# A fused transformer block: the mixing rounds issue in another order, and each chunk's rows are scattered a round later

## The chip, the cores and the metric

One core of one Trainium2 chip. The metric is the device time of one execution in microseconds (us). In the profile PE is TensorE (PEld its weight loads), DVE is VectorE, ACT is ScalarE, POOL is GpSimd and SP is SyncE.

## What is computed

The block has four layers, each with a residual and a layer norm before and after. The input is 32 sequences of 256 positions with 128 features. Cut to what matters:

```
x = x + ln(attention(ln(x)))            # 16 heads, causal, with a bonus per key
x = x + ln(wide(ln(x)))                 # 128 -> 512 gated, 512 -> 512 gelu, 512 -> 512 gelu, 512 -> 128
x = x + ln(recurrence(ln(x)))           # h = tanh(x_t Wi + bi + h Wh + bh) along axis 1
x = x + ln(experts(ln(x)))              # shared expert + one routed expert of 32

def wide(x):
    h = silu(x @ w1 * s1) * (x @ w2 * s2)
    h = gelu(h @ h1 * t1); h = gelu(h @ h2 * t2)
    return h @ w3 * s3

def experts(x):
    shared = silu(x @ sg) * (x @ su) @ sd
    logits = x @ gate_w
    owner, score = argmax(logits), sigmoid(max(logits))
    routed = swiglu of owner(x * score)
    return shared + routed
```

## The kernel before

The program has three stages: attention (to about 900 us in the trace), the mixing rounds (to about 1732 us), and the expert slots. The change touches only the second.

**Chunks and rounds.** The mixing stage (`mixing_experts`) works on 16 chunks of 512 rows (NC = 16, CHUNK = 512, four tiles of 128 rows, CT = 4). Every engine runs 21 rounds, k = 0 to 20 (`rounds`): eight written out, eight as a hardware loop of two, five written out. A round holds several chunks at once, each at another stage, and its arguments are their numbers: p = k is normed for the wide layer, a = k-1 goes through its first, gated layer, c = k-2 through its two 512 x 512 layers and the output, v = k-3 through the recurrence, h = k-4 through the norm behind the recurrence and the third residual sum, q = k-5 through the router, the shared expert and the placing of its rows. A letter is None where there is no such chunk. Rounds 5 to 15 hold all of them; round 16 has no p, round 17 no a, round 18 no c, round 19 no v, round 20 no h.

**Order of the work.** There is no scheduler. Each engine runs its own list in the order in which the code is written, and waits on semaphores. A wait holds up everything behind it on the same engine.

**PE in a round.** The four quarters of c's first 512 x 512 layer (`first_layer(0)` to `first_layer(3)`, L1228, L1230, L1237: 12 products of 128 x 512 each, the last four on the rounding remainder hT_low) are mixed with small things: the turning of xn4 (L1197, waits for ACT's copy of the state before it, hs), the router's logits (L1265), the shared expert's gate and up products in two halves (`shared(0)`, `shared(1)`, L1254), the turnings of xn2 and xn3 (L1197 too), the shared expert's down product (L1293), the recurrence's input product (L1300) and the counts for the placing (L1306 to L1311). `shared(1)` waits until DVE has emptied the two PSUM banks of `shared(0)`:

```
wait(pe, s["shid"], IC * q + m)
```

Behind that come, for each quarter m, a's first layer (L1322 to L1325) and c's second layer with 16 recurrence steps between the products (L1204), then the output (L1338) and the turning of the recurrence's state (L1350), which ends the round on PE.

**DVE in a round.** It starts with the norm of xn2 left from the end of the round before (L1519, chunk p), then for v: y (L1543), its statistics (L1510, L1514), its normed form (L1519, waits for POOL's brs_y), the second residual x (L1551) and its statistics. Then `shared(0)` (L1534, L1538: shid), xn2T_low (L1558), the norm of x (xn3, L1519), `shared(1)`, and the router's argmax (L1571 to L1582). The second half of the round holds the gated products (L1679, L1685), the gated rows, the norm of hs, the third sum (L1660), `place` (21 small instructions, L1616 to L1642), xn4, the statistics of x1c and the low parts (L1647).

**POOL in a round.** It makes one over the square root of the variance for each norm (`rstd`: L1144 scales, L1146 raises to -0.5), the rounding remainders of the gelu's output (`low_part`, L1139, four a round, for c's second layer) and, at the end, the scatter of q's rows to their places in DRAM (L1167: four indirect DMAs, one per tile). The scatter waits for the places, the gated rows and the shared expert's output of chunk q:

```
for k in range(CT):
    pool.indirect_dma_start(out=sorted_d[:, :], out_offset=bass.IndirectOffsetOnAxis(
        ap=pos_i[par][:, k:k + 1], axis=0), in_=row_buf[1 - par][:, k, :], in_offset=None)\
        .then_inc(s[f"placed{1 - par}"], 16)
```

`row_buf` has two buffers; DVE's third sum (L1660) writes the one that chunk h shares with chunk h-2, and waits until that chunk's rows are placed.

**ACT in a round.** Copies of the turned tiles out of PSUM (xn4T L1443, xn2T_high L1448, xn3T L1455, hs L1487), the gelu of each quarter (`middle`, L1423 and L1424), the tanh of the shared expert (L1430), the copy of its output (L1458) and of the router's top (L1463), and in the second half the tanh, gelu and recurrence steps (L1468, L1479, L1414). SP loads x1c and x1v and, in round 18, the experts' weights.

Of the kernel before, what the change touches and what calls it, by code (L numbers as in the profile page):

```python
# [906 lines left out]
def mixing_experts(nc, early, x1_d, mix, wgu, row_buf, sorted_d, gate_up, down, sh_gate_up, sh_down, out):  # L907
# [6 lines left out]
    with ExitStack() as ctx:  # L914
# [109 lines left out]
        def rounds(eng, step):  # L1024
            def row(k, par):
                return [v if not isinstance(v, int) or 0 <= v < NC else None for v in
                        (k, k - 1, k - 2, k - 3, k - 4, k - 5)] + [par]
# [44 lines left out]
        def _(sp):  # L1072
# [3 lines left out]
            def step(p, a, c, v, h, q, par):  # L1076
# [39 lines left out]
        def _(pool):  # L1116
# [31 lines left out]
            def step(p, a, c, v, h, q, par):  # L1148
# [5 lines left out]
                low_part(c, 1)  # L1154
                low_part(c, 2)
                low_part(c, 3)
# [5 lines left out]
                if q is not None:  # L1162
                    wait_apart(pool, s["pos"], q + 1, s["const"])
                    wait_apart(pool, s["rows"], q + 1, s["const"])
                    wait_apart(pool, s["sh_out"], q + 1, s["const"])
                    for k in range(CT):
                        pool.indirect_dma_start(out=sorted_d[:, :], out_offset=bass.IndirectOffsetOnAxis(  # L1167
                            ap=pos_i[par][:, k:k + 1], axis=0), in_=row_buf[1 - par][:, k, :], in_offset=None)\
                            .then_inc(s[f"placed{1 - par}"], 16)
# [24 lines left out]
        def _(pe):  # L1194
# [14 lines left out]
            def step(p, a, c, v, h, q, par):  # L1209
# [45 lines left out]

                if q is not None:
# [3 lines left out]
                first_layer(0)  # L1260
# [17 lines left out]
                first_layer(1)  # L1278
                if q is not None:
                    shared(1)  # L1280
                first_layer(2)
                if v is not None:
# [5 lines left out]
                    turn4(xn3[:], "p_xn3T")  # L1288
                if q is not None:
# [6 lines left out]
                first_layer(3)  # L1296
# [103 lines left out]
        def _(act):  # L1400
            act.wait_ge(s["const"], N_CONST)

            def step(p, a, c, v, h, q, par):
# [34 lines left out]

                if q is not None:
# [4 lines left out]
                middle(0)  # L1444
# [4 lines left out]
                shared(0)  # L1449
                middle(1)  # L1450
                shared(1)
                middle(2)
                if v is not None:
                    wait(act, s["p_xn3T"], v + 1)
                    act.activation(xn3T[:], turn[:, :], ACT.Copy).then_inc(s["xn3T"], 1)  # L1455
                if q is not None:
# [3 lines left out]
                middle(3)  # L1460
# [44 lines left out]
        def _(dve):  # L1505
# [18 lines left out]
            def step(p, a, c, v, h, q, par):  # L1524
# [16 lines left out]
                if v is not None:  # L1541
# [5 lines left out]
                    stats("y", lambda k: y[:, k, :], v)  # L1547
                    apply("y", y, lambda k: y[:, k, :], "yn", v)
# [261 lines left out]
```

## Time and profile before

| what | value |
|---|---|
| median of 3 runs | 1968.08 us (1967.4 to 1968.75) |
| the profiled execution, its own time | 1965.75 us |
| its span | 1964.0 us |
| PE busy | 1709.4 us (87%) |
| PEld busy | 1243.7 us (63%) |
| DVE busy | 1328.3 us (68%) |
| ACT busy | 887.3 us (45%) |
| POOL busy | 999.6 us (51%) |
| mean granted clock of PE | 0.956 |
| the DMA queues, share of 16 engines | 12.9% and 2.4% |

The span is one execution as the profiler saw it; the execution's own time is 1.75 us longer. Shares are averages over three stages with different limits, so they tell little about the mixing rounds alone. In a timeline row the idle time in brackets stands before the instruction, with what ended it; consecutive matmuls overlap, so the distance of two starts tells what one costs and the duration does not.

### The profile page before, as it was taken

What the parts mean: (1) busy time and instruction counts of PE and PEld (TensorE: products, weight loads), DVE (VectorE), ACT (ScalarE), POOL (GpSimd) and SP (SyncE); (2) the same over time, 40 slices, a digit from 0 to 9 for tenths busy, and PEclk for the clock granted to TensorE, in tenths of its full rate; (3) what the DMA queues carried; (4) which work ended last, traced back from release to release, by engine and by line L of the source; (5) the groups of instructions that cost most, each with busy time, mean ns of one, the idle gap of its engine ahead of it and who ended that gap; (6) DMA issues with size and microseconds to landing.
All of it is one profiled execution on the core that took longest, in us unless ns stands there. A gap on an engine that the chain in (4) does not pass through costs nothing. (4 is left out here: it accounts for less than half of the span.)

```text
span 1964.0 us, 43536 instructions
## 1 busy us (share of the span) xinstructions
PE 1709.4 (87%) x12768; PEld 1243.7 (63%) x12768; DVE 1328.3 (68%) x4113; ACT 887.3 (45%) x1955; POOL 999.6 (51%) x1825
## 2 busy tenths in 40 slices
PE   4999999999999999848899999999999998568884
PEld 3566666666666666536777777777777775335552
DVE  6777777777777777634556666666666656457774
ACT  2655555555555555414444444444444443123331
POOL 5777777777777777722223333333333332237775
PEclk8999999999999999969999999999999998679997
DMA  1011111111111112010110000000001005034431
GB/s 38 10 50 49 48 48 45 41 37 46 48 48 48 48 48 94 12 33 17 54 54 28 28 28 28 28 27 27 27 27 32 22 22 188 33 105 124 121 114 26
DMA packets 78237, 95.73 MB, mean 49 GB/s; under 512 B 7046, under 2 KB 62995, under 8 KB 78160
## 3 DMA queue, kind: packets, MB, share of 16 engines
q1 hardware_dynamic: 70992, 77.91, 12.9%
q0 software_dynamic: 7168, 16.87, 2.4%
q8 instruction: 40, 0.66, 0.1%
q14 instruction: 37, 0.30, 0.1%
HBM read 53.14 MB, written 43.69 MB: 49 GB/s over the span
## 5 line engine op out<-in xcount | busy, mean ns | idle before, releaser
L644 ACT ACTIVATE wgu<-score 128x384 f32<-128x384 f32 x512 | 223.1, 489 | 100.1 <-PE score L468 94.9
L313 POOL TENSOR_SCALAR_AFFINE_SELECT wgu<-wgu 128x512 f32<-128x512 f32 x256 | 164.3, 642 | 152.9 <-ACT wgu L644 144.3
L1228 PE MATMUL main<-hT_high,h_high 128*128 128x512 f32 x512 | 231.9, 453 | 0.9 <-ACT hT_high L1437 0.9
L1230 PE MATMUL main<-hT_high,h_low 128*128 128x512 f32 x512 | 204.6, 400 | 0.0
L491 PE MATMUL outp<-wgu 128*64 128x256 f32 (+1 forms) x2048 | 196.0, 334 | 0.9 <-POOL wgu L313 0.8
L491 PEld LDWEIGHTS outp<-wgu 128*64 128x64 f32 x2048 | 127.8, 137 | 58.1 <-issue 17.1
L1139 POOL TENSOR_TENSOR hT_low<-wgu,hT_high 128x512 fp32r<-128x512 f32 x64 | 82.2, 1285 | 151.5 <-ACT wgu L1424 151.4
L1679 DVE SCALAR_TENSOR_TENSOR th<-th,main 128x512 f32<-128x512 f32 x64 | 43.9, 685 | 156.3 <-ACT th L1468 156.3
L1237 PE MATMUL main<-hT_low,h_high 128*128 128x512 f32 x512 | 139.1, 393 | 0.1
L525 PE MATMUL back<-wout,wgu 128*128 128x128 f32 x1024 | 131.7, 283 | 0.0
L786 DVE TENSOR_TENSOR wgu<-spread,wgu 128x512 f32<-128x512 f32 x128 | 87.0, 680 | 61.1 <-PE spread L511 56.0
L1369 PE MATMUL main<-wgu,xgT 128*128 x192 | 105.8, 633 | 23.4 <-DVE xgT L1726 16.2
L525 PEld LDWEIGHTS back<-wout,wgu 128*128 128x128 f32 x1024 | 121.7, 195 | 4.9 <-issue 4.9
L1204 PEld LDWEIGHTS xi<-state,wh_sb 128*128 128x128 f32 x512 | 92.1, 193 | 41.5 <-ACT state L1414 26.1
L654 ACT ACTIVATE wgu<-outp 128x512 f32<-128x512 f32 x128 | 76.5, 598 | 88.7 <-PE outp L491 86.9
L1187 POOL DMA_INDIRECT out<-res,idx x96 | 101.0, 1053 | 24.9 <-issue 24.9
L1228 PEld LDWEIGHTS main<-hT_high,h_high 128*128 128x128 f32 x512 | 100.1, 196 | 18.7 <-issue 4.3
L1423 ACT ACTIVATE hT_high<-main,sc 128x512 fp32r<-128x512 f32 x64 | 44.0, 688 | 150.3 <-PE main L1237 133.9
L1237 PEld LDWEIGHTS main<-hT_low,h_high 128*128 128x128 f32 x512 | 96.6, 189 | 22.6 <-DVE hT_low L1647 0.8
L1230 PEld LDWEIGHTS main<-hT_high,h_low 128*128 128x128 f32 x512 | 99.6, 194 | 17.1 <-issue 4.9
L497 PE MATMUL total<-wgu,pick 128*32 128x256 f32 (+1 forms) x2048 | 110.4, 333 | 0.0
L1414 ACT ACTIVATE state<-xi,bias 128x32 f32<-128x32 f32 x256 | 73.2, 286 | 80.0 <-PE xi L1204 78.8
(270 smaller groups left out, 4244.3 us busy)
## 6 DMA issues: line engine op xcount, KB each, us to landing
sorted_d<-row_buf SPq DMA_DIRECT2D x26, 772.0 KB, 3.7
xg<-sorted_d SPq DMA_DIRECT2D x48, 386.0 KB
wgu<-in_gate_up SPq DMA_DIRECT2D x4, 2048.0 KB, 10.8
xa<-in_x SPq DMA_DIRECT2D x32, 128.0 KB, 3.5
xr<-in_x SPq DMA_DIRECT2D x32, 128.0 KB, 3.2
x_d<-x SPq DMA_DIRECT2D x32, 128.0 KB, 1.9
x1c<-x_d SPq DMA_DIRECT2D x16, 256.0 KB
x1v<-x_d SPq DMA_DIRECT2D x16, 256.0 KB
```

Source lines behind the costliest of these rows:

```text
L313: pool.affine_select(out=blocks, in_=blocks, compare_op=ALU.is_ge, fill=0.0, base=0, pattern=[[0, 4], [1, P]], channel_multiplier=-1).then ...
L491: m = pe.matmul(outp[DV * i:DV * (i + 1), p % 2, k * P:T], val[par][:, k, h, :], weights(h, k), start=(k == 0), stop=(k == 1), tile_positi ...
L497: m = pe.matmul(total[AUG * j:AUG * (j + 1), k * P:T], pick[:, g, :], weights(GH * g + j, k), start=(g == 0 and k == 0), stop=(g == GROUPS ...
L525: m = pe.matmul(back[:, i * P:(i + 1) * P], onT[1 - par][:, c, i * P:(i + 1) * P], wout[:, c, :], start=(c == 0 and i == 0), stop=(c == PA ...
L644: act.activation(prob[:, h // 2 % (RING // 2), :, h % 2, :], score[h % BANKS][:, 0:SC].rearrange("p (c q) -> p c q", q=P), ACT.Exp).then_i ...
L786: dve.tensor_tensor(o, spread[:], o, ALU.mult).then_inc(s["onT"], 1)
L1187: pool.indirect_dma_start(out=out_rows[:, :], out_offset=bass.IndirectOffsetOnAxis(ap=idx[k][:, n:n + 1], axis=0), in_=res[k][:, n, :], in ...
L1204: pe.matmul(xi[:, o:o + B], wh_sb[:], state[:, prev:prev + B], start=False, stop=(t == STEPS - 1), skip_group_check=True).then_inc(s["p_st ...
L1228: pe.matmul(main[m % 2][:, :], w[0][:, k, m * P:(m + 1) * P], src[0][:, k, :], start=(k == 0), stop=False)
L1230: pe.matmul(main[m % 2][:, :], w[1][:, k, m * P:(m + 1) * P], src[0][:, k, :], start=False, stop=False)
L1237: mm = pe.matmul(main[m % 2][:, :], w[0][:, k, m * P:(m + 1) * P], src[1][:, k, :], start=False, stop=(k == HC - 1))
L1369: pe.matmul(main[2 * (r % 2) + i][:, :], xgT[r % 2][:, i * P:(i + 1) * P], wgu[:, bass.ds(e, 1), :].rearrange("p o i -> p (o i)"), start=T ...
```

## The change

The number of instructions of each kind stays as it was, but for POOL's register moves. The order within a round changes on four engines.

- POOL: the scatter of a chunk moves from the end of its round k to the next round, where the chunk is called z = k-6. Two of its four DMAs come after low part 1, two after low part 2. Only the last chunk (q = 15, in round 20) is scattered at the end of its own round.
- PE: the first quarter of c's first layer comes before the turning of xn4, the second before the logits and `shared(0)`, the third between the turning of xn2 and `shared(1)`, and the last between the turning of xn3 and the down product.
- ACT: the gelus follow PE's new order; the tanh of `shared(0)` comes before the copy xn2T_high.
- DVE: the norm of xn2 moves from the end of the round into the next one (its chunk is then called a), behind the statistics of y. The norm of x comes before `shared(0)`; the router's argmax comes before `shared(1)`.

The core of the diff:

```diff
@@ -1024,7 +1024,7 @@
                 return [v if not isinstance(v, int) or 0 <= v < NC else None for v in
-                        (k, k - 1, k - 2, k - 3, k - 4, k - 5)] + [par]
+                        (k, k - 1, k - 2, k - 3, k - 4, k - 5, k - 6)] + [par]
             for k in range(8):
@@ -1145,28 +1145,35 @@

+            def scatter(z, par, k0, k1):
+                if z is None:
+                    return
+                wait_apart(pool, s["pos"], z + 1, s["const"])
+                wait_apart(pool, s["rows"], z + 1, s["const"])
+                wait_apart(pool, s["sh_out"], z + 1, s["const"])
+                for k in range(k0, k1):
+                    pool.indirect_dma_start(out=sorted_d[:, :], out_offset=bass.IndirectOffsetOnAxis(
+                        ap=pos_i[par][:, k:k + 1], axis=0), in_=row_buf[1 - par][:, k, :], in_offset=None)\
+                        .then_inc(s[f"placed{1 - par}"], 16)
+
                 if v is not None:
...
                 low_part(c, 1)
+                scatter(z, 1 - par, 0, CT // 2)
                 low_part(c, 2)
+                scatter(z, 1 - par, CT // 2, CT)
                 low_part(c, 3)
...
                     rstd("f", p)
-                if q is not None:
-                    wait_apart(pool, s["pos"], q + 1, s["const"])
-                    wait_apart(pool, s["rows"], q + 1, s["const"])
-                    wait_apart(pool, s["sh_out"], q + 1, s["const"])
-                    for k in range(CT):
-                        pool.indirect_dma_start(out=sorted_d[:, :], out_offset=bass.IndirectOffsetOnAxis(
-                            ap=pos_i[par][:, k:k + 1], axis=0), in_=row_buf[1 - par][:, k, :], in_offset=None)\
-                            .then_inc(s[f"placed{1 - par}"], 16)
+                if isinstance(q, int) and q == NC - 1:
+                    scatter(q, par, 0, CT)

@@ -1253,11 +1260,12 @@

+                first_layer(0)
                 if q is not None:
...
                     turn4(xn4[:], "p_xn4T")
-                first_layer(0)
+                first_layer(1)
                 if q is not None:
@@ -1275,10 +1283,9 @@
                     turn4(xn2[:], "p_xn2T")
-                first_layer(1)
+                first_layer(2)
                 if q is not None:
                     shared(1)
-                first_layer(2)
                 if v is not None:
@@ -1286,6 +1293,7 @@
                     turn4(xn3[:], "p_xn3T")
+                first_layer(3)
                 if q is not None:
@@ -1293,7 +1301,6 @@
                     m_.then_inc(s["p_sd"], 1)
-                first_layer(3)
                 if v is not None:
@@ -1436,28 +1443,28 @@

+                middle(0)
                 if q is not None:
...
                     act.activation(xn4T[:], turn[:, :], ACT.Copy).then_inc(s["xn4T"], 1)
-                middle(0)
+                middle(1)
+                shared(0)
                 if a is not None:
...
                     act.activation(xn2T_part[0][:], turn[:, :], ACT.Copy).then_inc(s["xn2T"], 1)
-                shared(0)
-                middle(1)
+                middle(2)
                 shared(1)
-                middle(2)
                 if v is not None:
...
                     act.activation(xn3T[:], turn[:, :], ACT.Copy).then_inc(s["xn3T"], 1)
+                middle(3)
                 if q is not None:
...
                                    main[2][:, :].rearrange("p (k d) -> p k d", d=D), ACT.Copy).then_inc(s["sh_out"], 1)
-                middle(3)
                 if q is not None:
@@ -1545,22 +1552,24 @@
                     stats("y", lambda k: y[:, k, :], v)
+                if a is not None:
+                    wait(dve, s["p_xn2T"], a)
+                    apply("f", xn2, lambda k: x1c[:, k, :], "xn2", a)
+                if v is not None:
                     apply("y", y, lambda k: y[:, k, :], "yn", v)
...
                     stats("x", lambda k: cur[:, k, :], v)
+                    wait(dve, s["p_xn3T"], v)
+                    apply("x", xn3, lambda k: cur[:, k, :], "xn3", v)
                 shared(0)
...
                                       ALU.subtract).then_inc(s["xn2T_low"], 1)
-                if v is not None:
-                    wait(dve, s["p_xn3T"], v)
-                    apply("x", xn3, lambda k: cur[:, k, :], "xn3", v)
-                shared(1)
                 if q is not None:
@@ -1581,6 +1590,7 @@
                     dve.wait_ge(s["onehot"], q + 1)
+                shared(1)

@@ -1690,9 +1700,6 @@
                     low_part(HC - 1)
-                if p is not None:
-                    wait(dve, s["p_xn2T"], p)
-                    apply("f", xn2, lambda k: x1c[:, k, :], "xn2", p)

```

On POOL, in a round with all chunks, from the norm of chunk p at the end of one round to the last low part of the next. The name hT_low is the remainder of c's hidden tile, sorted_d the DRAM buffer of placed rows, bve and brs with a letter the two steps of a norm's deviation. Before:

```order
L1146 TENSOR_TENSOR brs_f<-bve_f,pow_half 128x4
L1167 DMA sorted_d<-row_buf,pos_i 13312x386 x4
L1144 TENSOR_SCALAR bve_y<-bmv_y 128x4
L1146 TENSOR_TENSOR brs_y<-bve_y,pow_half 128x4
L1139 TENSOR_TENSOR hT_low<-wgu,hT_high 128x512
L1144 TENSOR_SCALAR bve_x<-bmv_x 128x4
L1146 TENSOR_TENSOR brs_x<-bve_x,pow_half 128x4
L1139 TENSOR_TENSOR hT_low<-wgu,hT_high 128x512 x3
```

And now:

```order
L1146 TENSOR_TENSOR brs_f<-bve_f,pow_half 128x4
L1144 TENSOR_SCALAR bve_y<-bmv_y 128x4
L1146 TENSOR_TENSOR brs_y<-bve_y,pow_half 128x4
L1139 TENSOR_TENSOR hT_low<-wgu,hT_high 128x512
L1144 TENSOR_SCALAR bve_x<-bmv_x 128x4
L1146 TENSOR_TENSOR brs_x<-bve_x,pow_half 128x4
L1139 TENSOR_TENSOR hT_low<-wgu,hT_high 128x512
L1155 DMA sorted_d<-row_buf,pos_i 13312x386 x2
L1139 TENSOR_TENSOR hT_low<-wgu,hT_high 128x512
L1155 DMA sorted_d<-row_buf,pos_i 13312x386 x2
L1139 TENSOR_TENSOR hT_low<-wgu,hT_high 128x512
```

The four scatters no longer stand ahead of the deviation of y; they stand in two pairs around the third low part, and they are those of the chunk before.

On DVE, from the last low parts of a round to the first shared pair of the next. xn written from x1c is xn2, from x it is xn3; th and shid are the shared expert's two steps. Before:

```order
L1647 TENSOR_TENSOR hT_low<-wgu,hT_high 128x512 x2
L1519 TENSOR_SCALAR xn<-x1c,bmv_f,brs_f 128x128 x4
L1543 TENSOR_TENSOR y<-yp,w3s 128x512
L1510 BN_STATS bstat_y<-y 128x6 x4
L1514 BN_AGGR bmv_y<-bstat_y 128x2 x4
L1519 TENSOR_SCALAR y<-y,bmv_y,brs_y 128x128 x4
L1551 TENSOR_TENSOR x<-y,x1v 128x512
L1510 BN_STATS bstat_x<-x 128x6 x4
L1514 BN_AGGR bmv_x<-bstat_x 128x2 x4
L1534 SCALAR_TENSOR_TENSOR th<-th,main 128x512
L1538 SCALAR_TENSOR_TENSOR shid<-main,th 128x512
L1558 TENSOR_TENSOR xn2T_low<-turn,xn2T_high 128x512
```

And now:

```order
L1550 TENSOR_TENSOR y<-yp,w3s 128x512
L1517 BN_STATS bstat_y<-y 128x6 x4
L1521 BN_AGGR bmv_y<-bstat_y 128x2 x4
L1526 TENSOR_SCALAR xn<-x1c,bmv_f,brs_f 128x128 x4
L1526 TENSOR_SCALAR y<-y,bmv_y,brs_y 128x128 x4
L1562 TENSOR_TENSOR x<-y,x1v 128x512
L1517 BN_STATS bstat_x<-x 128x6 x4
L1521 BN_AGGR bmv_x<-bstat_x 128x2 x4
L1526 TENSOR_SCALAR xn<-x,bmv_x,brs_x 128x128 x4
L1541 SCALAR_TENSOR_TENSOR th<-th,main 128x512
L1545 SCALAR_TENSOR_TENSOR shid<-main,th 128x512
L1571 TENSOR_TENSOR xn2T_low<-turn,xn2T_high 128x512
```

The norm of xn2 now stands between the statistics of y and its normed form, and the norm of x before the shared pair instead of behind it.

## Rows read from the trace of the kernel before

**Rows 1.** Waits of PE, 960 to 1760 us: who waited for whom, total us, times, longest.

```profile
PE main L1254 <- DVE shid L1538: 35.2, 14, 3.0
```

**Rows 2.** Timeline of PE: start us, duration us, what, count [idle before <-releaser].

```profile
1011.70 0.60 PE L1350 MATMUL turn<-ident,state 128*128 128x128 f32 x4
...
1057.31 0.60 PE L1350 MATMUL turn<-ident,state 128*128 128x128 f32 x4
...
1317.95 1.98 PE L1254 MATMUL main<-xn4T,sgu 128*128 128x512 f32 x4 [3.00 <-DVE shid L1538]
...
1366.56 3.01 PE L1254 MATMUL main<-xn4T,sgu 128*128 128x512 f32 x4 [2.99 <-DVE shid L1538]
...
1600.69 0.60 PE L1350 MATMUL turn<-ident,state 128*128 128x128 f32 x4
```

**Rows 3.** Windows: busy PE, PEld, DVE, ACT, POOL (instructions), granted clock, DMA share, GB/s.

```profile
1305.00:1354.00 49.00, 44.89 (x249) 35.86 (x248) 33.53 (x114) 21.30 (x45) 16.34 (x19) 1.00 0.09 27
...
1354.00:1404.00 50.00, 46.59 (x248) 36.65 (x248) 33.54 (x114) 20.73 (x45) 15.52 (x19) 0.97 0.08 26
```

**Rows 4.** Timeline of PE, the round that starts at 1304.41.

```profile
1304.41 0.60 PE L1350 MATMUL turn<-ident,state 128*128 128x128 f32 x4
...
1305.79 0.63 PE L1197 MATMUL turn<-ident,xn 128*128 128x128 f32 x4 [0.78 <-ACT hs L1487]
...
1306.17 0.48 PE L1228 MATMUL main<-hT_high,h_high 128*128 128x512 f32 x1
...
1309.00 0.97 PE L1265 MATMUL route<-gate_sb,xn4T 128*128 128x32 f32 x8
...
1311.61 0.60 PE L1197 MATMUL turn<-ident,xn 128*128 128x128 f32 x4
...
1332.81 1.09 PE L1237 MATMUL main<-hT_low,h_high 128*128 128x512 f32 x4
```

**Rows 5.** Timeline of PE and DVE, start of round 4 (no chunk in q yet).

```profile
969.40 0.60 PE L1350 MATMUL turn<-ident,state 128*128 128x128 f32 x4
...
969.76 0.48 PE L1228 MATMUL main<-hT_high,h_high 128*128 128x512 f32 x1
...
969.67 0.69 DVE L1543 TENSOR_TENSOR y<-yp,w3s 128x512 f32<-128x512 f32 x1 [0.73 <-PE yp L1338]
...
974.25 1.71 DVE L1551 TENSOR_TENSOR x<-y,x1v 128x512 f32<-128x512 f32 x1
...
978.77 2.92 DVE L1519 TENSOR_SCALAR xn<-x,bmv_x,brs_x 128x128 f32<-128x128 f32 x4 [0.91 <-POOL brs_x L1146]
```

**Rows 6.** Timeline of DVE, the round that starts at 1304.41.

```profile
1312.16 2.09 DVE L1519 TENSOR_SCALAR y<-y,bmv_y,brs_y 128x128 f32<-128x128 f32 x4 [3.17 <-POOL brs_y L1146]
...
1316.44 0.66 DVE L1534 SCALAR_TENSOR_TENSOR th<-th,main 128x512 f32<-128x512 f32 x1
...
1318.41 1.72 DVE L1519 TENSOR_SCALAR xn<-x,bmv_x,brs_x 128x128 f32<-128x128 f32 x4
...
1320.33 0.69 DVE L1534 SCALAR_TENSOR_TENSOR th<-th,main 128x512 f32<-128x512 f32 x1 [0.20 <-DVE xn L1519]
```

**Rows 7.** Timeline of POOL: around round 4 and that round.

```profile
972.06 1.01 POOL L1146 TENSOR_TENSOR brs_y<-bve_y,pow_half 128x4 f32<-128x4 f32 x1
...
1305.80 1.06 POOL L1167 DMA_INDIRECT sorted_d<-row_buf,pos_i  x1 [0.18 <-issue]
...
1324.15 1.28 POOL L1139 TENSOR_TENSOR hT_low<-wgu,hT_high 128x512 fp32r<-128x512 f32 x1 [4.87 <-ACT wgu L1424]
...
1329.11 1.29 POOL L1139 TENSOR_TENSOR hT_low<-wgu,hT_high 128x512 fp32r<-128x512 f32 x1 [3.69 <-ACT wgu L1424]
...
1352.89 1.27 POOL L1146 TENSOR_TENSOR brs_f<-bve_f,pow_half 128x4 f32<-128x4 f32 x1
```

**Rows 8.** Timeline of DVE, round 18.

```profile
1649.81 0.65 DVE L1534 SCALAR_TENSOR_TENSOR th<-th,main 128x512 f32<-128x512 f32 x1
...
1651.38 1.11 DVE L1519 TENSOR_SCALAR xn<-x,bmv_x,brs_x 128x128 f32<-128x128 f32 x4
```

More of the change, by code:

```diff
@@ L1074, in gate_up_weights, with step @@
                 sp.dma_start(wgu[:, e:e + 8, :], gate_up[e:e + 8].rearrange("e d i -> d e i")).then_inc(s["wgu"], 16)
-            def step(p, a, c, v, h, q, par):
+            def step(p, a, c, v, h, q, z, par):
                 if p is not None:
@@ L1146, in rstd, with step @@
                 pool.tensor_tensor(rs[n][:], ve[n][:], pow_half[:], ALU.pow).then_inc(s["rs" + n], 1)
-            def step(p, a, c, v, h, q, par):
+            def scatter(z, par, k0, k1):
[8 more added lines that the diff above has]
+                        .then_inc(s[f"placed{1 - par}"], 16)
+            def step(p, a, c, v, h, q, z, par):
                 if v is not None:
@@ L1207, in _, with step @@
             pe.wait_ge(s["const"], N_CONST)
-            def step(p, a, c, v, h, q, par):
+            def step(p, a, c, v, h, q, z, par):
                 slots = iter(range(STEPS))
@@ L1401, in _, with step @@
             act.wait_ge(s["const"], N_CONST)
-            def step(p, a, c, v, h, q, par):
+            def step(p, a, c, v, h, q, z, par):
                 slots = iter(range(STEPS))
@@ L1522, in apply, with step @@
                 dve.wait_ge(s[done], c + 1)
-            def step(p, a, c, v, h, q, par):
+            def step(p, a, c, v, h, q, z, par):
                 cur, old = x2[1 - par], x2[par]
```

## Prediction

> **What bounds the kernel now.** I read the waits of TensorE (PE) first, because only an idle PE can be removed by a reordering. Over the mixing rounds the largest one is L1254, the second shared product, which sits idle until DVE has written shid (L1538): 14 times, 35.2 us together [rows 1]. The timeline of PE then gives the rounds. Each ends with the turning of the recurrence state (L1350); with rounds counted from 0, round 5 runs from 1011.70 to 1057.31, 45.61 us, and rounds 6 to 16 from 1057.31 to 1600.69, 543.38 us or 49.40 each [rows 2]. All twelve do the same work (round 16 without the statistics of a new chunk), and round 5 alone has no chunk to scatter before it. In the others PE stops 3.0 us at L1254. That stop costs a second time: 49 us around the round that starts at 1304.41 show a granted clock of 1.00, the 50 us of the next one 0.97 [rows 3], a short time at 1.2 GHz in place of 2.4, and the L1254 behind its stop took 3.01 us where the other took 1.98 [rows 2]. Windows over the other rounds show 0.96 or 0.97 in six of the eleven.
>
> Where the stop comes from is in DVE and POOL. POOL issues four scatters (first 1305.80, 1.06 us) ahead of the reciprocal deviation of y [rows 7]; DVE, having nothing else in its order, waits 3.17 us for it before it can apply y [rows 6]. Then come x, its statistics, and only then the two instructions (L1534, L1538) on which PE waits. A smaller stop stands at the start of every round: the turning of xn4 waits for ACT's copy hs. It starts 1.38 us behind L1350 [rows 4], where the next matmul in round 4, with no such wait, starts 0.36 us behind [rows 5]: 1.02 us lost, in rounds 5 to 17.
>
> **The change, part by part.** Time is counted from the moment at which PE can issue behind L1350 ("the start").
>
> *A quarter of the wide layer ahead of the xn4 turning.* PE needs no hs for it, and ACT copies meanwhile. Its other inputs come from the round before. Saved: 1.02 us per round.
>
> *The shared product one quarter later.* By then PE has issued three quarters (1306.17 to 1309.00, 2.83 each), two turnings (0.38 each, 1305.79 to 1306.17), the logits and the first shared product (2.61 together, 1309.00 to 1311.61) [rows 4]: 8.49 + 0.76 + 2.61 = 11.86 us from the start.
>
> *When shid is there.* The scatters no longer precede y, but in DVE's order the apply of x now stands before shid. Round 4 shows this chain with no scatter and with a quarter issued first: y starts at 969.67, which is -0.09; the addition x takes 1.71 beside a low part of POOL; the apply of x starts at 978.77, which is 9.01 [rows 5]. Beside one low part that apply takes 1.72, 0.20 us pass before the L1534 behind it, and from the start of L1534 to the release of PE there are 1.51 (1316.44 to 1317.95) [rows 2, 6]: 9.01 + 1.72 + 0.20 + 1.51 = 12.44, which is 0.6 behind PE. One thing round 4 has not: the apply of xn2 (p's chunk, moved from the end of the round) now runs in DVE's wait for the deviation of y. It fits, being 1.1 us long as the apply of x alone is [rows 8], but a POOL power (brs) beside DVE work in SBUF takes 1.27 where an undisturbed one takes 1.01 [rows 7], and the small scaling before it suffers too. I take 0.6 us for both, and get a **remaining stop S of 1.2 us**. Its bounds: 0 if no instruction meets another (the apply of x then takes 1.1 and the addition 0.7), 2.8 if the apply of x takes its longest, 2.92 [rows 5], and y's apply 2.09 [rows 6]: 12.44 + 1.20 + 0.98 - 11.86. I choose nearer the low side, since round 4 is the same sequence measured.
>
> Here a page speaks against the change. Row first: y's apply took 2.09 us beside a low part [rows 6], against 1.11 for the same work undisturbed [rows 8]. By the Trainium skill (SBUF — State Buffer, Who interferes with whom) VectorE and GpSimd share a port pair which the first to issue holds for its whole instruction while the other fully blocks. That would lengthen three places of the new chain by a whole instruction each, and the sum would be that of rival B. The trace agrees in kind.
>
> *Sum for rounds 6 to 16.* A round without either stop is 45.61 - 1.02 = 44.59. With S it is 45.79, times 11 is 503.7, against 543.38: **39.7 saved**. This supposes that a stop of 1.2 us leaves the clock at 1.00, as the stops of 1 us in round 5 do.
>
> *Rounds 5 and 17.* They had only the hs stop and receive S: 2 x (1.02 - 1.2) = -0.4.
>
> *Round 18.* No wide layer runs there, so nothing hides DVE, and the apply of x moves ahead of the shared pair. L1534 started at 1649.81; the apply of x ran from 1651.38 for 1.11 [rows 8]. Now L1534 starts at about 1652.7: 2.9 us later, all on the path through PE to the recurrence. -2.9.
>
> *Rounds 3 and 4.* PE waits for the apply of x there already, and the rounding remainder xn2T_low (some 0.7 us, as L1534 with operands of its size) falls from before it to behind it: -0.7 each, -1.4.
>
> *Scatters.* POOL now has four in the gaps of 4.87 and 3.69 us around its low parts [rows 7]. Two at about 1.3 us, issue included, are 2.6 per gap. The shorter round takes some 3 us from both gaps together, 5.6 are left, 5.2 are used: nothing lost. The waits of a scatter are met a round earlier, so nothing is queued behind it for long; DVE's sum into the same buffer (L1660) waits for the landing, but it stands behind the second layer's start, which itself needs the low part that POOL issues after the last scatter. In rounds 19 and 20 nothing stands between, and the last scatter stays where it was: 0. The router's argmax moves before the second shared pair into time in which DVE waited; its result is read after the last quarter: 0. SP's load of the next chunk waits for xn2, about 2 us later, with most of a round to spare: 0.
>
> 39.7 - 0.4 - 2.9 - 1.4 = **35.0 us**. The profiled execution took 1965.75, its span 1964.0 and 1.75 around it; 1930.7 follows. The median of the runs is 2.3 us above that execution, so 1933.
>
> **Rivals.**
> A. *No stop is left (S = 0).* The shorter bound of every overlap holds. For it: in round 5 DVE applied y undisturbed. Against it: the addition of 1.71 us in round 4. 13 rounds x 1.2 more: 50.6 saved, 1917.5.
> B. *DVE's chain takes the old stop's place.* Every overlap blocks: S = 2.8, and the clock falls as before, which costs some 0.8 a round (49.40 less 44.59 is 4.8, of which the two stops are 3.0 and 1.0). 543.4 - 11 x 48.2 = 13.2, less 2 x 1.8 and 4.3: 5 saved, 1963. For it: the apply of x of 2.92 in round 4; against it: only one low part can meet it in a full round, since PE has a quarter and a product between them.
> C. *Slower: the scatters are stretched between the low parts.* POOL works in order, so a long scatter delays low parts 2 and 3. PE reads the last one at 1332.81 or later; it was complete at 1330.40 [rows 4, 7], 2.4 us of slack beside the 5.6 of gaps: 8.0 us for four scatters. Beyond 2.0 us per scatter PE waits, and beyond 2.0 + 3.2/4 = 2.8 the round is longer than before. The rows show 1.06 to 1.3; the strongest stretch in any row is 2.92 to 1.11, a factor of 2.6, which makes 3.3 each, 5.3 us of waiting, times 11 is 58 against 35 saved: 1991. By the Trainium skill (SBUF — State Buffer, A bandwidth-pool intuition that's wrong) a POOL-issued DMA of 620 ns takes about 3100 beside a VectorE copy, since its descriptors wait for the port; this case's row, a scatter of 1.06 beside the apply of xn2, does not show that.
> D. *The change doesn't do what it says:* the last quarter no longer covers the down product, so that ACT's copy of it or the argmax stops PE before the first layer's products. Against it: PE still has the input product and the ranks between. A stop of 1 us per round gives 13 less: 1946.
>
> **Chances and numbers.** Forecast, with S from 0.6 to 1.8 (13 rounds x 0.6 = 8 us to either side, 1925 to 1941): 0.58. A: 0.20. D: 0.08. B: 0.10. C: 0.04. Range: from A to D, 1916 to 1946, which leaves B and C outside. What a measurement of this kernel can tell from no change is 0.2%, 4 us. Faster needs under 1964.1: all but C and a part of B, 0.93; same 0.03; slower 0.04.
>
> **What would show it.** The L1254 wait, now on line 1261, should fall from 3.0 to about 1.2 us; the hs wait should be gone in rounds 5 to 17; rounds of about 45.8 us with clock 1.00 in every one; DVE's wait for the deviation of y at about 1.4 less the apply of xn2; scatters of 1.0 to 1.3 us; round 18 longer by 3. A wait of PE for hT_low would speak for C, one at the first layer's products for D. The forecast is wrong if rounds 6 to 16 average under 44.9 or over 46.7 us.

## The result, and the profile after

| | before | changed kernel |
|---|---|---|
| median | 1968.41 us (1964.99 to 1972.1, 6 runs) | 1954.47 us (1948.35 to 1960.03, 6 runs) |
| profiled execution, its span | 1965.75, 1964.0 us | 1948.35, 1946.6 us |
| PE busy (share of the span) | 1709.4 us (87%) | 1702.0 us (87%) |
| mean granted clock | 0.956 | 0.956 |

The ratio is 0.9931 [0.9912, 0.9951]: 14 us or 0.7% less, small but clear of the noise. The forecast was 1933, with a range up to 1946, so the gain is real but much smaller than forecast. Both profiled executions are low among their runs, and between them the gap is 17.4 us, where the sum had 35.0.

The waits of PE, 960 to 1760 us, in the changed kernel (answers to [rows 1]; line 1254 is now 1261, 1538 is 1545, 1197 is 1204):

```profile
PE main L1261 <- DVE shid L1545: 34.7, 16, 5.4
...
PE turn L1204 <- DVE xn2T_low L1571: 5.1, 1, 5.1
...
PE turn L1204 <- ACT hs L1494: 1.6, 2, 0.8
```

The stop for hs is gone from rounds 5 to 17, as planned. The stop at the second shared product is not: 34.7 us against 35.2. It is shorter in most rounds, but stands in more of them, and one, in round 18, took 5.4. The marks and stops one by one, in the timeline of PE (answers to [rows 2]):

```profile
1014.52 0.60 PE L1357 MATMUL turn<-ident,state 128*128 128x128 f32 x4
...
1060.84 0.60 PE L1357 MATMUL turn<-ident,state 128*128 128x128 f32 x4
...
1121.72 1.99 PE L1261 MATMUL main<-xn4T,sgu 128*128 128x512 f32 x4 [1.99 <-DVE shid L1545]
...
1299.13 0.60 PE L1357 MATMUL turn<-ident,state 128*128 128x128 f32 x4
1313.95 1.98 PE L1261 MATMUL main<-xn4T,sgu 128*128 128x512 f32 x4 [2.49 <-DVE shid L1545]
...
1360.91 3.50 PE L1261 MATMUL main<-xn4T,sgu 128*128 128x512 f32 x4 [2.33 <-DVE shid L1545]
...
1550.39 1.99 PE L1261 MATMUL main<-xn4T,sgu 128*128 128x512 f32 x4 [0.63 <-DVE shid L1545]
...
1582.71 0.60 PE L1357 MATMUL turn<-ident,state 128*128 128x128 f32 x4
```

Rounds 6 to 16 run from 1060.84 to 1582.71, 521.87 us or 47.44 each, where the forecast had 503.7. The eleven stops in them add up to 24.64, a mean of 2.24. Round 16, which loads no new chunk x1c, stops only 0.63. That is the first hint at the cause. The windows show what the stops did to the clock (columns as in [rows 3]):

```profile
1107.39:1154.02 46.63, 44.64 (x251) 35.87 (x249) 32.77 (x115) 21.08 (x44) 15.89 (x18) 1.00 0.09 29
1154.02:1203.31 49.29, 46.33 (x250) 36.40 (x249) 33.80 (x115) 21.07 (x44) 16.17 (x18) 0.97 0.08 28
...
1299.13:1346.25 47.12, 44.63 (x250) 35.87 (x249) 32.95 (x115) 21.08 (x44) 16.29 (x19) 1.00 0.08 28
1346.25:1394.71 48.46, 46.13 (x250) 36.46 (x249) 32.76 (x115) 21.08 (x44) 16.05 (x19) 0.96 0.08 27
```

Of rounds 5 to 17, each with a stop of up to 1.99 us stands at 1.00. From round 8 on, whose stop was 2.96, every second round up to 14 stands at 0.96 or 0.97, and those behind round 8 are 1.3 to 1.5 us longer than their neighbours, though their stops are only 2.3 to 2.6.

Now DVE, which PE waits for, in the round that starts at 1299.13 (answers to [rows 6]), and the loads that SP issues in it:

```profile
1299.45 0.69 DVE L1550 TENSOR_TENSOR y<-yp,w3s 128x512 f32<-128x512 f32 x1
...
1301.44 1.08 DVE L1526 TENSOR_SCALAR xn<-x1c,bmv_f,brs_f 128x128 f32<-128x128 f32 x4
1303.24 1.12 DVE L1526 TENSOR_SCALAR y<-y,bmv_y,brs_y 128x128 f32<-128x128 f32 x4 [0.71 <-POOL brs_y L1146]
1306.51 0.69 DVE L1562 TENSOR_TENSOR x<-y,x1v 128x512 f32<-128x512 f32 x1 [2.15 <-DMA x1v<-x_d]
...
1310.21 2.00 DVE L1526 TENSOR_SCALAR xn<-x,bmv_x,brs_x 128x128 f32<-128x128 f32 x4 [1.62 <-POOL brs_x L1146]
1312.41 0.69 DVE L1541 SCALAR_TENSOR_TENSOR th<-th,main 128x512 f32<-128x512 f32 x1 [0.20 <-DVE xn L1526]
```

```profile
1302.69 0.37 SPq L1079 DMA_DIRECT2D x1c<-x_d  x1
1303.31 0.37 SPq L1082 DMA_DIRECT2D x1v<-x_d  x1
```

The y chain does what was wanted: its norm starts 4.1 us behind the mark that opens the round instead of 7.75, and undisturbed (1.12 us instead of 2.09). Then DVE stands 2.15 us for x1v. SP runs its list in order. Ahead of the load of x1v stands the load of the next x1c, and that waits until DVE has normed the old x1c into xn2. The change moved this norm to 1301.44, so it ends at 1302.5 and both loads go out behind it. In the kernel before, in the round that starts at 1304.41:

```profile
1307.04 0.37 SPq L1079 DMA_DIRECT2D x1c<-x_d  x1
1307.81 0.22 SPq L1082 DMA_DIRECT2D x1v<-x_d  x1
```

```profile
1314.45 0.69 DVE L1551 TENSOR_TENSOR x<-y,x1v 128x512 f32<-128x512 f32 x1 [0.20 <-DVE y L1519]
```

Counted from the mark, the load of x1v goes out 4.18 us behind it, where it was 3.40: only 0.8 later. The larger part is that the y chain is now shorter: y's norm, behind which DVE wants x1v, ends 5.2 us behind the mark, where it was 9.8. An estimate from these rows: with the 3.2 us that the load takes here (1303.31 to 1306.51), the old issue time too would have been some 1.4 us late for the new y chain. So of the 2.15 us about 1.4 come from the earlier demand and 0.8 from the later norm; what both rest on is the place of x1v in SP's list.

POOL's scatters between the low parts (answers to [rows 7]), and round 18 on DVE and PE (answers to [rows 8]):

```profile
1311.53 1.10 POOL L1155 DMA_INDIRECT sorted_d<-row_buf,pos_i  x1 [0.17 <-issue]
1312.93 0.98 POOL L1155 DMA_INDIRECT sorted_d<-row_buf,pos_i  x1 [0.31 <-ACT wgu L1431]
1313.94 1.28 POOL L1139 TENSOR_TENSOR hT_low<-wgu,hT_high 128x512 fp32r<-128x512 f32 x1
```

```profile
1633.68 1.15 DVE L1526 TENSOR_SCALAR xn<-x,bmv_x,brs_x 128x128 f32<-128x128 f32 x4 [1.48 <-POOL brs_x L1146]
...
1636.40 3.78 PE L1261 MATMUL main<-xn4T,sgu 128*128 128x512 f32 x4 [5.42 <-DVE shid L1545]
```

A scatter takes what it took (median 0.98 us in both kernels), and PE waits for no low part. Round 18 grew from 31.58 to 33.93 us.

### The profile page after: what moved, and what is told of

The parts are those of the page before. It is cut to its first block and busy times, and to the rows that moved or that the text cites. A ratio compares the mean times of both kernels' runs of the same rounds, so it can differ in the third digit from the quotient of the medians.

```text
span 1946.6 us, 43587 instructions
## 1 busy us (share of the span) xinstructions
PE 1702.0 (87%) x12768; PEld 1243.3 (64%) x12768; DVE 1325.2 (68%) x4113; ACT 887.9 (46%) x1955; POOL 997.7 (51%) x1825
## 5 line engine op out<-in xcount | busy, mean ns | idle before, releaser
L1235 PE MATMUL main<-hT_high,h_high 128*128 128x512 f32 x512 | 224.0, 437 | 0.0
L786 DVE TENSOR_TENSOR wgu<-spread,wgu 128x512 f32<-128x512 f32 x128 | 87.0, 680 | 60.7 <-PE spread L511 55.6
L662 ACT ACTIVATE wgu<-back 128x512 f32<-128x512 f32 x128 | 76.4, 597 | 62.2 <-PE back L540 60.7
```

What stands on the lines that cost most here:

```text
L786: dve.tensor_tensor(o, spread[:], o, ALU.mult).then_inc(s["onT"], 1)
L1235: pe.matmul(main[m % 2][:, :], w[0][:, k, m * P:(m + 1) * P], src[0][:, k, :], start=(k == 0), stop=False)
```

## The experiments

Two theories came first. **L**: the load of x1v, queued on SP behind the norm of xn2, takes the gain. **P** (rival): DVE and POOL are in each other's way, the chain is long by itself, and the load only fills a gap. A third, here called **X**, shares the chain with L: the norm of x in front of the shared product takes a part (the expectation of e9 calls the two L+N). Then the parts of the change were run alone. Medians, and ratios to the kernel before with their 95% intervals:

| kernel | median us | ratio |
|---|---|---|
| e1: change, x1v loaded first | 1931.73 | 0.9819 [0.9805, 0.9832] |
| e2: change, shared product ahead of the norm of x | 1920.27 | 0.9773 [0.9756, 0.979] |
| e3: both | 1906.79 | 0.9693 [0.968, 0.9707] |
| e4: before, scatter move only | 1938.94 | 0.9863 [0.9848, 0.9878] |
| e5: before, PE and ACT order only | 1936.3 | 0.9847 [0.9829, 0.9865] |
| e6: before, x1v loaded first | 1963.97 | 0.9993 [0.9983, 1.0002] |
| e7: change, norm of xn2 back at the round's end | 1978.29 | 1.0073 [1.0056, 1.0091] |
| e8: e3 with round 19's norm earlier | 1905.29 | 0.9697 [0.9684, 0.971] |
| e9: change without its DVE order | 1929.48 | 0.98 [0.9754, 0.9846] |
| e10: before, DVE order only | 2034.43 | 1.0331 [1.0285, 1.0376] |

The kernel before had a median of 1966.23 us beside e1 to e4, 1965.22 beside e5 to e8 and 1970.26 beside e9 and e10, so medians of different groups compare only to within some 5 us; there the ratios say more.

### e1: x1v loaded first

On SP:

```diff
 def step(p, a, c, v, h, q, z, par):
+    if v is not None:
+        wait(sp, s["x2"], v)
+        sp.dma_start(x1v[:], chunk_of(x1_rows, v)).then_inc(s["xv"], 16)
     if p is not None:
         wait(sp, s["xn2"], p)
         sp.dma_start(x1c[:], chunk_of(x1_rows, p)).then_inc(s[f"xc{par}"], 16)
-    if v is not None:
-        wait(sp, s["x2"], v)
-        sp.dma_start(x1v[:], chunk_of(x1_rows, v)).then_inc(s["xv"], 16)
```

> The changed kernel with SP's two loads of a round in the other order: x1v (chunk v) ahead of the wait for xn2 and the load of x1c. Theory L (the load): in the changed kernel the addition that makes x waits 2.1 us for x1v in nearly every round, because SP issues that load behind its wait for xn2, which is now written later. Then the wait is gone here. The addition meets POOL's low part instead (1.7 us instead of 0.7), as in round 16 of the changed kernel, which has no chunk p and a stop of PE of 0.63 us at the second shared product. So stops of 0.6 to 1.3 us in rounds 5 to 17, rounds of 45.3 to 45.9 us, a granted clock of 1.00 in all of them, and a total near 1928 us, some 24 under the changed kernel. Rival P (DVE and POOL in each other's way): the chain is long by itself, the load only fills a gap; then the stop stays at 2.0 to 2.5 us, about half of the rounds lose clock, and the total stays within 4 us of the changed kernel's 1954.

1931.73 us: 23 us gained on the change by the order of two loads. The addition of x no longer waits for a load, only for the norm before it:

```profile
1291.74 1.12 DVE L1526 TENSOR_SCALAR y<-y,bmv_y,brs_y 128x128 f32<-128x128 f32 x4 [0.71 <-POOL brs_y L1146]
1293.05 1.50 DVE L1562 TENSOR_TENSOR x<-y,x1v 128x512 f32<-128x512 f32 x1 [0.20 <-DVE y L1526]
```

```profile
PE main L1261 <- DVE shid L1545: 20.4, 16, 4.1
```

Stops in rounds 6 to 16 are 0.63 to 1.72 us, the clock is 1.00 over all of them, and they take 504.0 us (1058.58 to 1562.61) where the forecast had 503.7. Theory L holds, and P, which had the total stay within 4 us of 1954, falls. The load does not give back its 2.15 us in full, since the addition now meets a low part of POOL (1.50 instead of 0.69).

### e2 and e3: the shared product ahead of the norm of x, alone and with e1

On DVE; between the two places stands xn2T_low:

```diff
-    wait(dve, s["p_xn3T"], v)
-    apply("x", xn3, lambda k: cur[:, k, :], "xn3", v)
     shared(0)
...
+    if v is not None:
+        wait(dve, s["p_xn3T"], v)
+        apply("x", xn3, lambda k: cur[:, k, :], "xn3", v)
```

> The changed kernel with DVE's first shared pair and the remainder xn2T_low back ahead of the norm of x, SP as it was. Theory L: x1v is still late by 2.1 us, but the pair no longer waits for the deviation of x (1.5 to 1.6 us) and its application (2.0 us), so shid is there some 3.6 us earlier than in the changed kernel, 1.2 us before PE asks: no stop in rounds 5 to 17, rounds of 44.6 to 44.9 us, clock 1.00, round 18 back from 33.9 to about 31, total near 1918. Rival P: the application of x, now later, meets low parts and scatters; the stop moves to the turning of xn3, 1 us or more a round, total 1930 or above.

1920.27, 34 us below the change. The stop at the second shared product is gone from rounds 5 to 17. I had expected no stop at all in them; the rest of the wait moves to the down product, where it is small:

```profile
PE main L1301 <- DVE shid L1545: 9.1, 13, 1.4
```

> Both edits: x1v loaded first, and the shared pair with xn2T_low ahead of the norm of x. Theory L: shid is early by 2 us or more, PE has no stop left, and the loads' order adds nothing to the second edit: within 3 us of it, near 1917 us, rounds 5 to 16 of 44.6 us each at a clock of 1.00. Rival P: 2 us or more apart from the second edit alone in the direction of the longer chain, or stops of PE at the turning of xn3.

1906.79, 13.5 us below e2, where I had expected almost nothing more. The marks of PE at the ends of rounds 5 and 16:

```profile
1054.26 0.60 PE L1357 MATMUL turn<-ident,state 128*128 128x128 f32 x4
...
1542.66 0.60 PE L1357 MATMUL turn<-ident,state 128*128 128x128 f32 x4
```

Eleven rounds of exactly 44.40 us with no stop that the trace shows. In e2 these rounds took 497.25 against 488.40: the late load still delayed the second shared pair, for which the down product waits. Another 3.8 us lie before round 6, where PE waits for the norm of x itself: 4.9 and 4.2 us in rounds 3 and 4 of e2, 3.5 and 3.1 in e3. So X holds as well. The two costs come one after the other in one chain, and a shorter chain pays only until PE no longer stops: alone the edits give 23 and 34 us, together 48 and not 57.

### e4, e5 and e6: the parts alone

e4 takes POOL's part of the change alone (the scatter diff shown above), on the kernel before. e5 takes that of PE and ACT alone, of which this is the PE half; the gelus on ACT follow it:

```diff
+first_layer(0)
...
-first_layer(0)
+first_layer(1)
...
-first_layer(1)
+first_layer(2)
...
-first_layer(2)
...
+first_layer(3)
...
-first_layer(3)
```

e6 is e1's edit on the kernel before.

> The kernel before with nothing changed but the scatters: a round later, in pairs around the third low part. The deviation of y no longer waits for four scatters. Theory L and my sum: y is applied 1.8 us earlier (3.17 us of wait become 1.4), the addition then meets a low part less; the stop at the second shared product falls from 3.0 to between 0.5 and 1.3 us, and the clock stays at 1.00, so 11 rounds give 2 to 2.8 us each: 22 to 30 us, total 1939 to 1946. Rival P: DVE meets POOL elsewhere and the stop stays above 2 us: total above 1955. If the scatters are stretched between the low parts, PE waits for hT_low and the total is above 1968.

1938.94:

```profile
PE main L1261 <- DVE shid L1545: 17.8, 14, 1.9
...
PE turn L1204 <- ACT hs L1494: 11.3, 15, 0.8
```

The stop falls to half and the one for hs stays. From round 8 to 15 the stop is 1.35 to 1.85 us, more than the 0.5 to 1.3 expected, but the clock is 1.00 in rounds 4 to 17. DVE now waits 1.54 us for brs_y instead of 3.17.

> The kernel before with nothing changed but the order on PE and ACT: the quarters of the wide layer one place earlier among the small products, the scatters and DVE as before. Theory L and my sum: the hs stop goes (1.0 us in 13 rounds) and PE asks for shid at 11.9 us from its start where it asked at 10.0, while shid comes at 13.1 as before; a stop of 1.2 to 1.5 us is left, the clock stays at 1.00: rounds near 45.9, some 35 us saved, total 1929 to 1937. Rival P: moved work of PE and ACT meets DVE elsewhere (rank products, xn2T_low) and the stop stays above 2 us: total above 1945.

1936.3. The hs stop is gone. The stop at the shared product is 1.2 us where it was 3.0, since PE asks a quarter later; behind it stands one of equal size for the norm of x, which I had not expected, so rounds 6 to 16 take 47.2 us each and not near 45.9:

```profile
1304.70 1.98 PE L1254 MATMUL main<-xn4T,sgu 128*128 128x512 f32 x4 [1.20 <-DVE shid L1538]
1307.90 0.66 PE L1197 MATMUL turn<-ident,xn 128*128 128x128 f32 x4 [1.22 <-DVE xn L1519]
```

> The kernel before with SP's two loads of a round in the other order. No row of it shows DVE waiting for x1v, so theory L expects no change: 1966 us within 3. Rival: the loads' order is worth something by itself (less contention for DMA or an earlier statistic): more than 4 us.

1963.97, no difference: in the kernel before the load had time to spare, as the forecast said. It is the change that made it late, by wanting it earlier and by issuing it later.

Each of the two parts alone, e4's and e5's, gains more (27 and 30 us by the ratios) than the whole change (14). So a part of the change must cost.

### e7: the norm of xn2 back at the round's end

On DVE, from behind the statistics of y to the end of the round before:

```diff
-    if a is not None:
-        wait(dve, s["p_xn2T"], a)
-        apply("f", xn2, lambda k: x1c[:, k, :], "xn2", a)
...
+    if p is not None:
+        wait(dve, s["p_xn2T"], p)
+        apply("f", xn2, lambda k: x1c[:, k, :], "xn2", p)
```

> The changed kernel with the norm of xn2 back at the end of the round, SP as it was. Theory L: xn2 is written at 2.1 us instead of 3.1, so x1v is issued a microsecond earlier and meets the addition in time or nearly so; but y now stands behind the norm and starts 2.1 us later, so y's chain takes the place of the load: shid at 14 to 14.7, a stop of 2.2 to 2.8 us, half of the rounds at a lower clock, total within 5 us of the changed kernel. Rival P says that the place of the norm in the round is what costs, through the port: then this is 8 us or more faster than the changed kernel.

1978.29, 24 us slower than the change: a miss. The load is in time again, but DVE is not. Timeline of DVE in the round that starts at 1306.04, then PE's stop and the window of the round:

```profile
1307.40 1.11 DVE L1526 TENSOR_SCALAR xn<-x1c,bmv_f,brs_f 128x128 f32<-128x128 f32 x4 [0.98 <-POOL brs_f L1146]
1308.55 0.69 DVE L1550 TENSOR_TENSOR y<-yp,w3s 128x512 f32<-128x512 f32 x1
...
1312.17 2.05 DVE L1526 TENSOR_SCALAR y<-y,bmv_y,brs_y 128x128 f32<-128x128 f32 x4 [1.54 <-POOL brs_y L1146]
```

```profile
1321.84 3.78 PE L1261 MATMUL main<-xn4T,sgu 128*128 128x512 f32 x4 [3.47 <-DVE shid L1545]
```

```profile
1306.04:1356.97 50.93, 47.46 (x251) 37.32 (x249) 34.04 (x115) 21.07 (x44) 15.98 (x19) 0.93 0.08 26
```

The norm stands in front of y with its own wait, so y starts 2.51 us behind the mark instead of 0.32; y's norm then falls onto a low part (2.05 instead of 1.12 us). Those 3.1 us outweigh the 2.15 of the load by 1.0, which is the growth of the stop (3.47 against 2.49). I had set the two equal. The larger half is the clock: with stops of 3.5 to 3.9 us the three rounds from 1306.04 on stand at 0.93 each, with none at 1.00 between, and take 51.1 us where the change takes 47.8 on average. Over rounds 6 to 16 the stops grow by 13.4 us and the time by 28.8. The first such stop did not do this, though: round 8 (1156.36 to 1204.86) stopped 3.86 us and stood at 1.00. With the norm of x ahead of the shared product, as here, the move of this norm pays; it brings a late load only because SP's list was left as it was.

### e8: the tail

e3, and in the round where h is the last chunk the norm xn4 ahead of `place`, since PE waits 14 us for it there:

```diff
-place()
+late = isinstance(h, int) and h == NC - 1
+if not late:
+    place()
 if h is not None:
...
     apply("e", xn4, lambda k: third[:, k, :], "xn4", h)
+if late:
+    place()
```

> Both edits of the third run, and in round 19 alone DVE norms the last chunk (xn4) before it places chunk 14's rows. PE waits 14 us for that norm at the start of round 20 and does nothing else; the placing takes 5.3 us and nothing needs it so early. Expected: 5 us less than the third run, 1902; if the chain through the placing or the scatter of chunk 14 sets the end instead, no change.

1905.29, where 5 us less than e3 were expected: 1.5 us below e3 by the medians, no difference by the ratios (0.9697 and 0.9693). PE's stop in round 20 falls from 13.99 to 10.33 us, but then it waits for what `place` makes:

```profile
1642.19 1.11 PE L1204 MATMUL turn<-ident,xn 128*128 128x128 f32 x4 [10.33 <-DVE xn L1526]
1647.53 1.92 PE L1273 MATMUL route<-gate_sb,xn4T 128*128 128x32 f32 x8 [4.23 <-DVE pos_i L1653]
```

The wait was moved, not removed.

### e9 and e10: the DVE order undone, and alone

e9 is the change with DVE's norms where they were (e2's and e7's edits together); e10 is the kernel before with DVE's part of the change alone.

> The changed kernel with VectorE's order put back (the norm of xn2 at the round's end, the norm of x behind the first shared product and the low part of xn2T), scatters and PE/ScalarE order as in the change. Theory L+N (the DVE order costs by two things: the x1v load queued behind the later norm of xn2, and the norm of x ahead of the shared product): the shared product is ready about 3 us earlier than in the run with the norm at the end, so the stop at it is gone or under 0.5 us and moves to the down product; the y chain still starts 2.5 us after the round mark, so rounds are about 1 us longer than with the shared product ahead alone (44.4 to 45.5): 45.3 to 46.5 us, 1925 to 1938 us in all, faster than the change (1954). Rival (the DVE order is what pays, scatters and PE order alone can't): 1955 or more.

1929.48, 25 us faster than the change. In rounds 6 to 16 the stops at the shared product are gone, those at the down product are 0.8 to 1.5 us, and the rounds take 45.5 to 46.9.

> The kernel before with VectorE's order of the change alone (norm of xn2 a round later in the gap of the y chain, norm of x ahead of the first shared product). Theory L+N: slower than before. The norm of x (1.7 to 2.7 us) and its wait for brs_x (1.6 us) now stand ahead of the shared product, the y chain starts 2.2 us sooner but the wait for brs_y behind SCATTERS on GpSimd (3.2 us) stays: stop at the shared product 3.5 to 5 us instead of 2.5, 1975 to 2000 us. Rival (the DVE order is neutral or gains by itself): 1968 or less.

2034.43, slower than before by 65 us (by the ratio), more than the 7 to 32 I had expected. POOL (first fence), DVE and PE in the round that starts at 1394.94:

```profile
1396.28 1.05 POOL L1167 DMA_INDIRECT sorted_d<-row_buf,pos_i  x1 [0.18 <-issue]
...
1401.56 1.04 POOL L1146 TENSOR_TENSOR brs_y<-bve_y,pow_half 128x4 f32<-128x4 f32 x1
```

```profile
1395.15 0.68 DVE L1543 TENSOR_TENSOR y<-yp,w3s 128x512 f32<-128x512 f32 x1
...
1402.71 2.03 DVE L1519 TENSOR_SCALAR y<-y,bmv_y,brs_y 128x128 f32<-128x128 f32 x4 [4.47 <-POOL brs_y L1146]
...
1408.66 1.98 DVE L1519 TENSOR_SCALAR xn<-x,bmv_x,brs_x 128x128 f32<-128x128 f32 x4 [1.62 <-POOL brs_x L1146]
```

```profile
1412.39 3.78 PE L1254 MATMUL main<-xn4T,sgu 128*128 128x512 f32 x4 [6.95 <-DVE shid L1538]
```

y starts at once, and its norm still begins 7.8 us behind the mark, as in the kernel before (7.75), since the four scatters stand ahead of brs_y. The early start is worthless while the scatters are there. The norm of x and its wait (1.62 + 1.98 + 0.22 = 3.8) are paid in full: the stop grows from 3.00 to 6.95.

So the DVE order costs 25 us on top of the other two parts and 65 without them. Split by its halves, from the medians: the norm of x ahead of the shared product costs 34 (change against e2) or 49 (e7 against e9), the move of the norm of xn2 saves 24 (e7 to change) or 9 (e9 to e2; 5 by the ratios, whose intervals overlap, so this one is not clear of the noise), and 23 or 13.5 more once x1v is loaded first.

## Why the prediction was wrong

- **What bounds the rounds:** right. Shortening PE's idle time is what each faster kernel does, and e3, without those stops, has the fastest rounds. (The old stops in rounds 6 to 16 are 2.5 to 3.0 us, together 31.7, not 3.0 each.)
- **The quarter ahead of the xn4 turning, 1.02 us a round:** right. The hs wait is 1.6 us in all. A round with no stop is 44.40 in e3 against the 44.59 worked out.
- **When PE asks:** right. In the round from 1299.13 it is 1313.95 - 2.49 - 1299.49 = 11.97 us from the start (forecast 11.86).
- **When shid is there:** this failed, and with it the forecast, at "SP's load of the next chunk waits for xn2, about 2 us later, with most of a round to spare: 0". That is true of x1c (it goes out 3.6 us behind the mark, where it was 2.6, so even less than 2 later). I had followed the wait to the load that it guards and not to the next one in SP's list, x1v, which DVE needs in the same round, and I had read the slack of the loads in the kernel before, where DVE wanted x1v 9.8 us behind the mark and not, as now, 5.2. The chain forecast at 12.44 plus 0.6 took 14.46. The terms: the addition of x could start 0.57 us later than in round 4 (forecast 0.6; y's norm ends 0.41 later, and the 0.2 that e1 and e7 show between the two were not in round 4); the load adds 1.95 (forecast 0); the addition takes 0.69 (forecast 1.71, as it no longer meets the low part); the wait for brs_x and the norm of x take 0.5 more (2.00 instead of 1.72 in the norm). Without the load (e1) the sum came out at 504.0 us for rounds 6 to 16, and the whole at 1931.73 against 1933.
- **"A stop of 1.2 us leaves the clock at 1.00":** right as it stands (e1), but the stop was 2.24 on average, and the sum had no term for what a longer one does to the clock. The 18.2 us missing from rounds 6 to 16 are 11 x 1.04 = 11.4 of stop and 6.7 of clock, but for 0.4: a round of this kernel without its stop is 44.63, not 44.59.
- **Rounds 3 and 4:** forecast 1.4 lost. PE's waits in them grew by 4.1 us: 5.6 and 5.1 for xn2T_low, where it waited 3.5 and 3.1 for the norm of x. The late load again: in e1 they are 4.4 and 3.9, 1.7 more than before and close to the forecast. The start of round 5 moved by only 2.8 (1011.70 to 1014.52), because this execution came to the output of round 2 2.3 us earlier (921.26 against 923.54). That is no gain of the change: e3 and e8, which are alike up to there, differ by 2.6 at that place.
- **Rounds 5 and 17:** forecast 0.4 lost, measured 1.0. **Round 18:** forecast 2.9, measured 2.35. Right in place and nearly in size. PE starts the second shared pair 11.05 us behind the mark there, where it was 8.32; it stops 5.42, not 1.45, since it also asks 1.2 us earlier.
- **Scatters, "nothing lost":** right. **Rival C** falls: 0.96 to 1.25 us each, median 0.98, and no wait of PE for a low part. The Trainium skill (SBUF — State Buffer, A bandwidth-pool intuition that's wrong) would have a POOL-issued DMA stretched about fivefold, from 620 ns to 3100, beside a VectorE copy; here, beside norms and additions, no scatter shows it (1.10 us beside the norm of x at 1311.53).
- **Rival D** falls: no stop at the first layer's products. **Rival A** (no stop left) is the neighbour of what e2 and e3 reach, but the change does not.
- **Rival B** came nearest: S of 2.8 with a lower clock, 1963. Its outcome was half right (2.24, and the clock), its mechanism not: y's norm ran undisturbed and only the norm of x was stretched. By the Trainium skill (SBUF — State Buffer, Who interferes with whom) one of the two engines would wait while the other holds the port; 2.00 us beside a low part of 1.29, against 1.11 alone, agrees in kind. It cost 0.9 us against the undisturbed norm and 0.3 against the 1.72 of the forecast, not the three whole instructions of B.

The balance against the profiled execution, mark by mark: rounds up to 5 +3.5 (of which -2.3 lie before round 3), rounds 6 to 16 -21.5, rounds 17 and 18 +2.7, the rest of the program -2.1, together -17.4.

The forecast also took the change as it came. It priced the norm of x ahead of the shared product (1.72 + 0.20 and the wait for brs_x) as a part of the chain, and never asked what the chain would be without it. In e3 the order that the change gave up, with the rest of it kept, ends 48 us lower.

## What to carry to other kernels

Where an instruction is moved, list for every queue that waits on it not the guarded transfer alone but all that is queued behind it, and ask of each who needs it first: here two loads in the wrong order cost 23 us. Count its slack against the new schedule, not the old one: here the user of the load came 4.6 us earlier and the load itself only 0.8 later. A change of several parts is best run part by part and as the whole without each: the scatter move and the PE order gained 27 and 30 us alone, and the DVE order gave 25 of the 39 us back that they gained together. Work that no one waits for soon (the norm of x) belongs behind what PE waits for next, also where the engine has a gap for it.

## What the hardware showed that I had not expected

- **Clock:** stops of up to 1.99 us at one place of a 46 us round left the granted clock at 1.00. A round with one of 2.96 stood at 0.97, and from then on, with stops of 2.3 to 2.6, every second round stood at 0.96. The length of the stop alone does not tell it. In e7 a round with a stop of 3.86 stood at 1.00, the next at 0.97, and only the six behind these, with 3.5 to 4.0, at 0.93 each. In e6, with stops of 2.5 to 3.05, one round stood at 0.93 and the next at 1.00. In e10, with stops of 6.1 to 7.2, rounds 6 to 16 all stood at 0.94. Over rounds 6 to 16 the changed kernel lost 6.3 us beyond its 24.6 us of stops, e7 21.8 beyond 38.0. Why the clock alternates was not tried.
- **The tail's clock:** rounds 19 and 20 and the hand-over, the same work in both, took 60.2 us at a mean clock of 0.67 in the changed kernel and 66.4 at 0.55 in e3. In the other kernels they took 59.8 to 63.3, but for e1, which had 66.4 as well. Windows from the end of round 18 to the first expert tile, changed kernel and e3:

```profile
1659.28:1719.52 60.24, 22.24 (x104) 13.86 (x105) 25.30 (x101) 6.84 (x12) 12.06 (x14) 0.67 0.13 48
```

```profile
1615.10:1681.50 66.40, 29.94 (x104) 18.13 (x105) 25.30 (x101) 6.85 (x12) 11.97 (x14) 0.55 0.12 43
```

Six microseconds that go with no edit: e6 and e8 load x1v first as e1 and e3 do and took 60.7 and 59.8. The profiled executions of e1 and e3 are the slowest of their five (1934.25 and 1910.4), so this is likely a part of the spread between executions of one kernel; it was not tried. It is enough to hide the gain of an edit like e8's, which is in this stretch: at the same 0.67 e8 took 59.8, the changed kernel 60.2.
